# Seven, six and three: a new split of sixteen scan inputs over three engines of one core

## The reference

```python
def step(h, inp):
    u_t, d_t, B_t, C_t = inp
    dA = jnp.exp(d_t[..., None] * As)
    h = h * dA + (d_t * u_t)[..., None] * B_t[:, :, None, :]
    y = jnp.einsum('bkcn,bkn->bkc', h, C_t)
    return (h, y)
```

## Time and profile before

| | |
|---|---|
| median of 3 runs | 1898.98 us (1898.94 to 1900.81) |
| profiled execution, its own time | 1899.25 us |
| its span, first to last instruction | 1897.4 us |
| mean granted clock of TensorE | 0.918 of full |
| scan stretch of the first pair | 148.0 to 703.0 us |
| scan stretch of the second pair | 905.6 to 1453.8 us |
| rows of B and C loaded | 864 transfers of 128 KB |

### The profile page before, as it was taken

One profiled execution on the slowest core, in us unless ns is written; L12 is line 12 of the kernel. 1 busy time (PEld: TensorE's weight loads), 2 busy tenths in 40 slices (PEclk: granted clock), 3 DMA queues, 4 the chain that ended last, 5 costly groups with the idle time before them and its releaser, 6 DMA issues.

```text
span 1897.4 us, 17753 instructions
## 1 busy us (share of the span) xinstructions
PE 1552.7 (82%) x5004; PEld 767.2 (40%) x5005; DVE 1463.4 (77%) x1570; ACT 1081.1 (57%) x1960; POOL 1306.8 (69%) x501
## 2 busy tenths in 40 slices
PE   5866878877888887986687788888888749999997
PEld 2323433433443434532343343344333335555554
DVE  6588999998999997657999999999996752323232
ACT  3777777876777754377777787777774211111110
POOL 1458999998999981145899999999996122222221
PEclk9877999998999998887799999999998869999999
DMA  3184435426434320218443543443432661111110
GB/s 120 45 300 171 131 113 172 137 97 211 133 96 144 106 98 29 77 57 301 163 132 106 172 139 97 136 146 104 132 104 97 224 236 35 43 45 47 50 50 14
DMA packets 107360, 228.15 MB, mean 120 GB/s; under 512 B 18302, under 2 KB 31137, under 8 KB 103440
## 3 DMA queue, kind: packets, MB, share of 16 engines
q1 hardware_dynamic: 102160, 213.02, 34.2%
q0 software_dynamic: 5120, 14.21, 2.4%
HBM read 184.13 MB, written 44.60 MB: 121 GB/s over the span
## 4 chain that ended last, share of the span: by engine, by line
PE 35%; DVE 26%; POOL 18%; issue 14%; ACT 4%; DMA 2%; SPq 1%; DVEq 0%; POOLq 0%; ACTq 0%
DVE arena L921 17%; POOL arena L472 16%; PE psum L1372 10%; PE psum L1391 5%; DVE arena L897 4%; PE psum L1146 3%; PE psum L1223 3%; PE psum L1196 3%; POOL arena L457 2%; PE psum L1300 1%; PE psum L1249 1%; PE psum L1319 1%; DMA arena<-bc_dram 1%; PE psum L1158 1%; PE psum L1382 1%
## 5 line engine op out<-in xcount | busy, mean ns | idle before, releaser
L472 POOL TENSOR_TENSOR arena<-arena 128x1536 f32<-128x1536 f32 x256 | 876.1, 3460 | 23.7 <-ACT arena L707 15.8
L1223 PE MATMUL psum<-arena,ident 128*128 128x512 f32 x1536 | 743.0, 620 | 72.7 <-POOL arena L472 72.7
L921 DVE TENSOR_TENSOR_SCAN arena<-psum,arena 128x512 f32<-128x512 f32 x528 | 615.0, 1233 | 0.0
L698 ACT ACTIVATE psum<-arena 128x512 f32<-128x512 f32 x528 | 364.2, 690 | 264.3 <-DVE arena L921 254.3
L1223 PEld LDWEIGHTS psum<-arena,ident 128*128 128x128 f32 x1536 | 283.0, 198 | 386.8 <-issue 258.9
L921 DVE TENSOR_TENSOR_SCAN arena<-arena,psum 128x512 f32<-128x512 f32 x240 | 288.5, 1240 | 20.0 <-PE psum L1249 15.3
L1249 PE MATMUL psum<-ident,arena 128*128 128x128 f32 x960 | 152.9, 287 | 141.2 <-DVE arena L921 141.2
L675 ACT ACTIVATE arena<-arena 128x192 f32<-128x192 f32 x640 | 234.7, 440 | 0.0
L1249 PEld LDWEIGHTS psum<-ident,arena 128*128 128x128 f32 x960 | 117.7, 146 | 271.2 <-issue 132.9
L457 POOL TENSOR_TENSOR arena<-arena 128x1536 f32<-128x1536 f32 x64 | 221.1, 3454 | 4.0 <-issue 4.0
L897 DVE TENSOR_TENSOR arena<-psum,arena 128x1536 f32<-128x1536 f32 x112 | 194.4, 1736 | 21.1 <-ACT psum L683 12.2
(11 more groups left out here) (160 smaller groups left out, 1478.7 us busy)
## 6 DMA issues: line engine op xcount, KB each, us to landing
arena<-bc_dram SPq DMA_DIRECT2D x864, 128.0 KB, 3.0
step_dram<-arena SPq DMA_DIRECT2D x16, 1536.0 KB, 8.1
arena<-step_dram SPq DMA_DIRECT2D x32, 768.0 KB, 7.9
arena<-in_x SPq DMA_DIRECT2D x8, 1536.0 KB, 9.3
arena<-in_w SPq DMA_DIRECT2D x6, 1876.0 KB, 10.7
t_dram<-arena SPq DMA_DIRECT2D x16, 386.0 KB, 3.8
arena<-in_w SPq DMA_DIRECT2D x4, 1536.0 KB, 13.4
z_dram<-arena SPq DMA_DIRECT2D x2, 1536.0 KB, 5.2
```

The source lines that it names most:

```text
L472: g.tensor_tensor(x, x, Cs[c % C_RING][:, None, :].to_broadcast([P, CG, HALF]), ALU.mult)\
L698: a.activation(dA[e % 2], steps[g % 2][0][:, j, :], ACT.Exp, scale=A[:, KORDER[kk], j, n:n + 1]).then_inc(s_dA, 1)
L921: v.tensor_tensor_scan(x, decay, given, 0.0 if first else state[:, n, j:j + 1], ALU.mult, ALU.add).then_inc(s_scan, 1)
L1223: ins = pe.matmul(bank[j], ident[:, :], X3[c % RING][:, j, :], start=False, stop=(n == NS - 1), skip_group_check=True)
```

## The change

MAKER has a new order. GpSimd makes three inputs in place of four (states 0, 7, 12; before 0, 4, 8, 12), VectorE six in place of seven (1, 3, 5, 9, 11, 13; before also 7), ScalarE with TensorE seven in place of five (2, 4, 6, 8, 10, 14, 15; before 2, 6, 10, 14, 15). SCALED places the 56 scalings of a group (before 40). The columns of B that ScalarE copies for its scalars (`b_columns`) are now seven, by two instructions as before.

```diff
-MAKER = "PDADPDADPDADPDAA"
-BY_SCALAR = (2, 6, 10, 14, 15)
+MAKER = "PDADADAPADADPDAA"
+BY_SCALAR = (2, 4, 6, 8, 10, 14, 15)
 LAST_D = 13
-SCALED = {15: ((2, 0, 3),), 0: ((2, 3, 8),), 2: ((6, 0, 2),), 4: ((6, 2, 8),), 6: ((10, 0, 5),),
-          8: ((10, 5, 8), (14, 0, 3)), 10: ((14, 3, 8),), 12: ((15, 0, 6),), 13: ((15, 6, 8),)}
+SCALED = {15: ((2, 0, 3),), 0: ((2, 3, 8),), 1: ((4, 0, 2),), 2: ((4, 2, 8),), 3: ((6, 0, 2),),
+          4: ((6, 2, 8),), 5: ((8, 0, 3),), 6: ((8, 3, 5),), 7: ((8, 5, 8),), 8: ((10, 0, 6),),
+          9: ((10, 6, 8),), 10: ((14, 0, 6),), 11: ((14, 6, 8),), 12: ((15, 0, 6),), 13: ((15, 6, 8),)}
...
                 def b_columns(i):
                     c, cols = ND * p + i, bank[0].rearrange("p (t b n) -> p t b n", t=TT, b=4)[:, :, 0:2, :]
                     a.wait_ge(s_btps, c + 1)
-                    a.activation(BT[:, PREP[i], :, :, 0:4], cols[:, :, :, 2:15:4], ACT.Copy)
-                    a.activation(BT[:, PREP[i], :, :, 4], cols[:, :, :, 15], ACT.Copy).then_inc(s_bt, 1)
+                    a.activation(BT[:, PREP[i], :, :, 0:5], cols[:, :, :, 2:11:2], ACT.Copy)
+                    a.activation(BT[:, PREP[i], :, :, 5:7], cols[:, :, :, 14:16], ACT.Copy).then_inc(s_bt, 1)
```

## The result

The changed kernel is slower by 0.41%: 1905.74 us median against 1898.71 for the kernel before (20 runs of each, 1900.25 to 1915.67 and 1892.36 to 1905.48), ratio 1.0041, 95% interval 1.0027 to 1.0054. The forecast was 1916. The sign and the range (1884 to 1924) held; the loss is 7 to 8 us and not 17.

What follows compares the result with a forecast made beforehand. GpSimd was taken to set the pace, VectorE just behind. With state 4 late, the scan stretches summed to 1120.2 us against 1103.2; 17.0 on top of 1899.25 gave 1916, range 1884 to 1924.

Steps and rivals of the forecast that it cites:

- What bounds the kernel; the sums of work: Scan stretches: GpSimd sets the pace at 68.2 us a group, VectorE just behind at 65.1 and 67.9.
- ScalarE at state 2: Four more scalings delay the previous group's evacuation, ending at G (group start) + 13.2, or + 14.6 in groups 3, 4, 7.
- TensorE behind it: The opening of new sums waits for the evacuation and precedes state 4's transposes: scans at G + 19.2 even at full clock.
- The clock at the opening: TensorE falls to its lower clock in 14 groups: opening 4.4 us, not 2.6; state 4's scans start at G + 21.0.
- Rival 1: The first rival: TensorE keeps full clock at the opening; 25 us less, 1891, faster; chance 0.20.
- From state 4 to the end of a group: Nine GpSimd instructions 30.8, then 6.3 until state 14's scans, then 7.6 for states 14 and 15: 44.7 us.
- rival 3: TensorE does not fall at state 10, so the wait there is milder; 14 us less, 1902, no change; chance 0.10.
- The groups one by one: Groups of a pair: 68.6, 69.1, 69.3, 70.5, 70.7, 69.1, 69.3 and 72.0; 558.6 us together.
- The load of x: Group 4 of the first pair: state 7's row of B lands late, GpSimd wants it earlier; 3.0 us lost.
- State 7's input, "0 to 0.2 a group; 0 taken": GpSimd finishes this input 6.9 us after state 4, when VectorE needs it; at most 0.2 us a group.
- The sign: Slower, chance 0.63; state 4 ending 1.1 us earlier in each of 16 groups would give no change.

Runs made afterwards that it cites:

- y_first: The changed kernel with the evacuation of step 2 moved ahead of that step's six scalings; 1898.87 us, 0.9989 of the kernel before.
- keep_early: The changed kernel with the kept state copied ahead of exponential 1 in steps whose state isn't ScalarE's; 1897.64 us, 0.9992 of the kernel before.
- spread: The changed kernel with evacuation ahead of step 2's scalings, kept state ahead of exponential 1, and state 4's scalings taken earlier; 1885.77 us, 0.9930.
- h4_spread: The kernel before with state 4 given to ScalarE, evacuation and kept state moved earlier, three of state 4's scalings out of step 2; 1898.64 us, 0.9999.
- h8_both: The kernel before with state 8 given to ScalarE, evacuation ahead of step 2's scalings and kept state ahead of exponential 1; 1883.64 us, 0.9915.
- h4: The kernel before with state 4 alone moved from GpSimd to ScalarE and TensorE; 1913.95 us, 1.0076 of the kernel before.
- the same two edits: Evacuation ahead of step 2's scalings and kept state ahead of exponential 1; on the changed kernel 1896.24 us, on the kernel before 1896.72 us.

## Why the prediction was right in sign and wrong in size

**What bounds the kernel; the sums of work.** Right in the main. GpSimd was full, and the change frees it. In second groups VectorE was as full (busy 68.38 us of the 68.44 of group 1), where the forecast counted 67.9. And the waits of 0.85 and 0.67 in the earlier trace rows stand in front of the second and third scan of state 14, not of 14 and 15; the 1.5 us stay the same.

**ScalarE at state 2.** Right: the evacuation ended at G + 13.0 in group 6, forecast G + 13.2. `y_first` shows that its place matters.

**TensorE behind it.** Right: in group 6 state 4 ended at 586.0, G + 24.4, forecast 24.6, after a wait of 1.96 for a forecast of some 2.

**The clock at the opening** is the step that failed: the stretch of TensorE between state 2's transposes and the opening "lasts from 573.9 to 577.9, 4.0 us, in all groups but the first of a pair", and "I take the fall in all of them". Seven of 14 openings fell: the six of groups 2, 4 and 6, and one of the eight of groups 1, 3, 5 and 7. Below, the gap is the time from the end of the last addition to the opening. In groups 1 and 5 state 2 itself had to wait, 1.05 to 1.08 us in three of them and 1.55 in the fourth (1.08 at 641.72 in group 7), since its transposes stand behind the addition of state 15, which waits for GpSimd (0.55 us between the additions at 634.91 and 638.30 there). The transposes began at G + 10.8 (11.3 in the fourth), not at 9.2, and the gap shrank to 2.4 us. In groups 3 and 7 the gap was 3.6 us and the clock held, apart from group 3 of the second pair, whose gap was 5.3 and whose length was 70.48, forecast 70.5. With 7 falls fewer, the sum that the forecast used for its first rival is half due: 7 x 1.8 = 12.6 less, 1916.3 - 12.6 = 1903.7. That this is near the measured 1905.74 is partly luck: the seven groups without a fall came out only 7.0 us under the forecast, 1.0 each, since state 2's own wait stands in the place of state 4's. Rival 1 was not a case beside the forecast; the kernel is both at once, group by group.

**From state 4 to the end of a group** (44.7) came out at 44.2, with two errors that nearly cancel. The product of 4 waits for the kept state, +1.0, a term that the forecast left out; the nine instructions ended 31.8 after state 4 and not 30.8. Against that the addition of state 10 ran at full clock (617.87, 2.84 us after a wait of 2.57, forecast 4.2), so 4.8 and not 6.3. In the kernel before this addition fell in six of the eight first groups. The forecast kept it in all eight, and its rival 3 took it away; here it fell in one, group 2 of the second pair. That is 7 x 1.5 = 10.5 us less than forecast against 8 x 1.0 more for the kept state.

```profile
1096.65 4.33 PE L1224 MATMUL psum<-arena,ident 128*128 128x512 f32 x6 [2.41 <-POOL arena L473]
```

There state 14 waited 1.63 us, and the group took 70.32.

**The groups one by one.** Forecast less measured, both pairs: groups 0: 1.0; 1 and 5: 2.6; 2 and 6: 1.0; 3: 1.7; 4: 1.5; 7: 2.8; together 10.6. That is 17.0 against 6.4: 7.0 in the seven groups whose opening didn't fall, and the other 3.6 almost all in first groups.

**The load of x**: right. VectorE's wait moved to state 7's scans and has the size that the forecast gave it (3.0):

```profile
456.03 3.45 DVE L922 TENSOR_TENSOR_SCAN arena<-psum,arena 128x512 f32<-128x512 f32 x3 [3.27 <-POOL arena L458]
```

**State 7's input, "0 to 0.2 a group; 0 taken"**: wrong, 0.9 in each first group, through the kept state.

**The sign.** "a state 4 that ends 1.1 us earlier in each of 16 groups gives no change": `y_first` took away waits of 1.8 to 2.1 us in seven groups, 14 us or 0.9 a group, and the kernel came out even with the one before. That the time rose at all isn't owed to state 4's wait alone: `keep_early`, which leaves that wait in place, is even too, and the forecast had the kept state's delay at 0.1 us. So the right sign rests in part on a cost that the forecast left out. What it did not see either is that the same shares win 0.7% with another order (`spread`).

**Open.** What remains between `h4_spread` and `h8_both` was read from group lengths and not taken apart by a run of its own. What state 7's move to GpSimd is worth alone, and how much of `h4`'s loss is TensorE's clock at states 10 and 14, no run tells. Why one late opening falls and the next does not is not settled.

## What to carry to other kernels

When work is spread over more in-order queues, look first at which position the new pieces take in each queue, and choose as the item to move one whose successors have slack: here state 8 won 0.5% and state 4 lost 0.8% with the same sums, in the order as it was. An order that frees an engine earlier brought nothing that can be told while that engine was full (0.9983 [0.9961, 1.0005]), and the same two edits brought 0.6% in the changed kernel, where it has less to do. And a price seen in three places of a trace (a clock that fell) is a chance, not a constant: look at a second execution before it is multiplied by fourteen.

## What the hardware showed

Whether TensorE falls to its lower level is not set by the program alone. Read on TensorE's timelines of all 17 kernels (outside each pair's first group, and without three where a record is missing) by how long after the end of the last addition the opening began, with only twelve transposes and waits in between: of 163 openings that began 2.34 to 3.07 us after it, none took over 2.84 us. Of 72 that began 3.23 us after it or later, 40 took 4.1 us or more. Among these a longer stretch did not make a fall surer: 16 of 24 fell at 3.3 to 3.5 us, none of 11 at 3.5 to 3.7, and 20 of 31 later ones. The same place fell in one execution of the changed kernel and not in the next. The Trainium skill says that a transpose doesn't count as activity for the clock gate (TensorE: Matmul & The Clock Gate, Part 4: PE-mode transpose). The rows agree in that every opening that fell came behind a stretch of transposes and waits. They do not let one say which of these stretches brings a fall.
